# A Swin block with convolution on one core: shorter norm on VectorE, ScalarE's x1 copies moved up, other MLP banks, GpSimd's x1 rows ahead of the shifts

## The reference

```python
def _layer_norm(x, g, b):
    mu = x.mean(-1, keepdims=True)
    var = ((x - mu) ** 2).mean(-1, keepdims=True)
    return (x - mu) / jnp.sqrt(var + EPS) * g + b
...
xn = _layer_norm(x, ln1_g, ln1_b)
xs = jnp.roll(xn, shift=(-SHIFT, -SHIFT), axis=(1, 2))
...
qkv = wins @ qkv_w + qkv_b
attn = softmax(q * scale @ k.T + bias + mask)   # per window and head
out = roll_back(windows_back(attn @ v) @ proj_w + proj_b)
x = shortcut + out
y = _layer_norm(x, ln2_g, ln2_b)
y = jax.nn.gelu(y @ fc1_w + fc1_b)
x = x + (y @ fc2_w + fc2_b)
...
y = depthwise3x3(relu(x)) + dw_bias
y = (y @ pw_kernel + pw_bias) * inv + (beta - moving_mean * inv)
```

## Time and profile before

| | |
|---|---|
| median of 3 runs | 5511.71 us (5501.87 to 5517.33) |
| the profiled execution, its own time | 5513.41 us |
| its span | 5511.6 us |
| busy PE, DVE, ACT, POOL | 96%, 94%, 92%, 70% of the span |
| mean busy share of the DMA engines | about a tenth; 39 GB/s |
| granted clock of TensorE, over the span | 0.995 of full speed |
| chain that ended last, by engine | DVE 37%, POOL 28%, PE 23%, ACT 6%, issue 5% |

### The profile page before, as it was taken

The page is one execution under the profiler, slowest core; times in us unless marked ns, Lnnn a source line. Parts: engine busy times, 40 slices in busy tenths (PEclk is TensorE's granted clock), DMA queues, the critical chain, the costliest instruction groups (busy, mean ns, idle before and its releaser), DMA issues.

```text
span 5511.6 us, 202651 instructions
## 1 busy us (share of the span) xinstructions
PE 5283.0 (96%) x81186; PEld 3763.1 (68%) x81186; DVE 5190.1 (94%) x13517; ACT 5061.2 (92%) x10782; POOL 3841.7 (70%) x4105
## 2 busy tenths in 40 slices
PE   5999999999999999999999999999999999999998
PEld 3666666666666666666666666666666766666665
DVE  4999999999999999999999999999999999999998
ACT  4999999999998999999999999999999999999996
POOL 3677777777776777777777777777776777777773
PEclk9999999999999999999999999999999999999998
DMA  1111111111111111111111111111111111111111
GB/s 26 38 39 40 39 40 40 40 40 41 40 39 38 41 38 41 40 39 40 39 40 40 40 40 41 40 39 40 39 40 39 40 40 41 39 41 40 39 40 27
DMA packets 304318, 216.10 MB, mean 39 GB/s; under 512 B 233255, under 2 KB 274712, under 8 KB 303384
## 3 DMA queue, kind: packets, MB, share of 16 engines
q1 hardware_dynamic: 303384, 203.13, 13.9%
HBM read 77.81 MB, written 77.07 MB: 28 GB/s over the span
## 4 chain that ended last, share of the span: by engine, by line
DVE 37%; POOL 28%; PE 23%; ACT 6%; issue 5%; SPq 1%; DVEq 0%; DMA 0%; POOLq 0%; ACTq 0%
DVE acc L873 13%; PE bank L441 12%; POOL prob L985 11%; POOL prob L976 11%; POOL x1n L1002 6%; DVE stats L891 5%; DVE smax L841 5%; DVE prob L832 5%; DVE x L928 4%; PE bank L549 4%; ACT xT L685 3%; ACT x1T L638 3%; PE bank L478 3%; PE bank L424 1%; PE bank L459 1%
## 5 line engine op out<-in xcount | busy, mean ns | idle before, releaser
L873 DVE SCALAR_TENSOR_TENSOR acc<-ymap,taps,acc 96x784 f32<-96x784 f32 (+2 forms) x2176 | 2157.9, 996 | 54.8
L991 POOL TENSOR_TENSOR rstd<-var_eps,minus_half 112x7 f32<-112x7 f32 x512 | 936.2, 1828 | 1091.5 <-DVE var_eps L906 1091.5
L441 PE MATMUL bank<-x1T,w 96*128 96x448 f32 (+1 forms) x3072 | 1136.5, 506 | 87.2 <-ACT x1T L638 85.9
L976 POOL TENSOR_TENSOR prob<-prob,smax 128x392 f32<-128x392 f32 x768 | 829.4, 1080 | 430.3 <-DVE smax L841 430.3
L459 PE MATMUL bank<-hT,w 128*96 128x448 f32 (+1 forms) x3072 | 1097.9, 493 | 0.0
L649 ACT ACTIVATE hT<-bank,bfc 128x448 f32<-128x448 f32 (+1 forms) x1536 | 826.0, 575 | 54.9 <-PE bank L441 36.0
L1002 POOL TENSOR_SCALAR xn<-x_in,minus_mean,rstd 112x96 f32<-112x96 f32 x768 | 834.5, 1096 | 45.2 <-POOL offset L994 45.1
L441 PEld LDWEIGHTS bank<-x1T,w 96*128 96x128 f32 x3072 | 545.4, 191 | 411.2 <-issue 193.6
L459 PEld LDWEIGHTS bank<-hT,w 128*96 128x96 f32 x3072 | 466.9, 163 | 342.8 <-issue 166.0
L985 POOL TENSOR_TENSOR prob<-prob,srec 128x392 f32<-128x392 f32 x768 | 630.6, 848 | 0.4 <-DVE srec L850 0.4
L703 ACT ACTIVATE ymap<-bank,cols 96x448 f32<-96x448 f32 (+4 forms) x544 | 494.3, 921 | 73.3 <-PE bank L459 73.3
(11 more groups left out here) (101 smaller groups left out, 10464.0 us busy)
## 6 DMA issues: line engine op xcount, KB each, us to landing
out<-o_tile SPq DMA_DIRECT2D x256, 210.0 KB, 2.5
x_in<-in_x SPq DMA_DIRECT2D x256, 168.0 KB, 2.9
x_in<-in_x SPq DMA_DIRECT2D x256, 126.0 KB, 2.8
k<-qk SPq DMA_DIRECT2D x512, 49.0 KB, 1.9
ymap<-ymap SPq DMA_DIRECT2D x256, 85.5 KB, 2.0
out<-o_tile SPq DMA_DIRECT2D x256, 84.0 KB, 2.5
hT<-in_L_conv_rel_bias SPq DMA_DIRECT2D x49, 0.6 KB
x1T<-in_L_conv_fc_w SPq DMA_DIRECT2D x1, 144.0 KB, 2.4
```

The lines of the kernel that those rows point to most:

```text
L441: pe.matmul(bank[(1, 2, 5)[m]][:, 0:n * PT_], w1[:, m * 128:(m + 1) * 128], x1T[:, first * PT_:(first + n) * PT_], start=True, stop=True). ...
L873: last = dve.scalar_tensor_tensor(out=dst, in0=src, scalar=taps[:, i:i + 1], in1=dst, op0=ALU.mult, op1=ALU.add)
L976: pool.tensor_tensor(p, p, m, ALU.subtract).then_inc(shifted, 1)
L991: pool.tensor_tensor(b["rstd"][:], b["var_eps"][:], minus_half[0:PT_], ALU.pow)\
```

## The change

The norm: DVE keeps four of its seven small instructions (difference, deviation with the epsilon, between, and their sum `squares`), scaled by C throughout, and the factor sqrt(C) that this leaves goes into the weights, once, ahead of the loop. POOL takes over the sum of the halves' means and minus the mean, behind the statistics (`stats_done`), ahead of its root. The rows that POOL normalises are now x times rstd plus offset. ACT copies x1T ahead of the second xT copy. `hidden` writes banks 2, 5, 1 in turn, and its waits move along with them. POOL normalises its x1n rows ahead of the shifts.

```diff
@@ hidden, TensorE
                     if i == 0:
+                        wait(pe, x1t_ready, nth(t - 1, 2, 0))
+                    elif i == 1:
+                        wait(pe, x1t_ready, nth(t - 1, 2, 1))
+                    elif i == 2:
                         wait(pe, xt_ready, nth(t + 2, 2, 1))
-                    elif i == 1:
-                        wait(pe, x1t_ready, nth(t - 1, 2, 0))
                     elif i > 2:
                         wait(pe, h_ready, nth(t - 1, 6, i - 3))
-                    pe.matmul(bank[(1, 2, 5)[m]][:, 0:n * PT_], w1[:, m * 128:(m + 1) * 128],
+                    pe.matmul(bank[(2, 5, 1)[m]][:, 0:n * PT_], w1[:, m * 128:(m + 1) * 128],
@@ step, ScalarE
                 probs_turned(t + 1, 2)
+                x1_turned(t + 1)
                 x_turned(t + 1, 1)
-                x1_turned(t + 1)
                 attention_out(t + 1)
@@ norm_stats, VectorE
-                dve.tensor_tensor(b["sum"][:], st[:, :, 1], st[:, :, 4], ALU.add)
                 dve.tensor_tensor(b["diff"][:], st[:, :, 1], st[:, :, 4], ALU.subtract)
-                dve.tensor_tensor(b["dev"][:], st[:, :, 2], st[:, :, 5], ALU.add).then_inc(parts_done[which], 1)
+                dve.scalar_tensor_tensor(out=b["dev"][:], in0=st[:, :, 2], scalar=C * LN_EPS, in1=st[:, :, 5],
+                                         op0=ALU.add, op1=ALU.add).then_inc(parts_done[which], 1)
                 wait(dve, parts_done[which], nth(s, 1, 0))
-                dve.tensor_scalar(b["minus_mean"][:], b["sum"][:], -0.5, None, ALU.mult)
-                dve.scalar_tensor_tensor(out=b["between"][:], in0=b["diff"][:], scalar=0.25, in1=b["diff"][:],
-                                         op0=ALU.mult, op1=ALU.mult)
-                dve.tensor_scalar(b["within"][:], b["dev"][:], 1.0 / C, eps, ALU.mult, ALU.add)\
-                    .then_inc(halves_done[which], 1)
+                dve.scalar_tensor_tensor(out=b["between"][:], in0=b["diff"][:], scalar=0.25 * C, in1=b["diff"][:],
+                                         op0=ALU.mult, op1=ALU.mult).then_inc(halves_done[which], 1)
                 wait(dve, halves_done[which], nth(s, 1, 0))
-                dve.tensor_tensor(b["var_eps"][:], b["between"][:], b["within"][:], ALU.add)\
+                dve.tensor_tensor(b["squares"][:], b["between"][:], b["dev"][:], ALU.add)\
                     .then_inc(ln_ready[which], 1)
@@ root and rest, GpSimd
+                wait(pool, stats_done[which], nth(s, 1, 0))
+                pool.tensor_tensor(b["sum"][:], b["stats"][:, :, 1], b["stats"][:, :, 4], ALU.add)\
+                    .then_inc(summed[which], 1)
+                wait(pool, summed[which], nth(s, 1, 0))
+                pool.tensor_scalar(b["minus_mean"][:], b["sum"][:], -0.5, None, ALU.mult)
                 wait(pool, ln_ready[which], nth(s, 1, 0))
-                pool.tensor_tensor(b["rstd"][:], b["var_eps"][:], minus_half[0:PT_], ALU.pow)\
+                pool.tensor_tensor(b["rstd"][:], b["squares"][:], minus_half[0:PT_], ALU.pow)\
...
-                    last = pool.tensor_scalar(dst[:, j], src[:, j], b["minus_mean"][:, j:j + 1],
-                                              b["rstd"][:, j:j + 1], ALU.add, ALU.mult)
+                    last = pool.tensor_scalar(dst[:, j], src[:, j], b["rstd"][:, j:j + 1],
+                                              b["offset"][:, j:j + 1], ALU.mult, ALU.add)
@@ step, GpSimd
                 second_scale(t)
+                second_rest(t)
                 shift(t + 1, 0)
                 shift(t + 1, 1)
                 shift(t + 1, 2)
-                second_rest(t)
```

More of the change, by code:

```diff
@@ L50 @@
 LN_EPS, BN_EPS = 1e-4, 1e-3
+ROOT_C = float(C) ** 0.5
 MASKED = -100.0
@@ L158, in swin_conv_kernel @@
                (("stats", (WS, 6)), ("sum", (WS,)), ("diff", (WS,)), ("dev", (WS,)), ("between", (WS,)),
-                ("within", (WS,)), ("minus_mean", (WS,)), ("var_eps", (WS,)), ("rstd", (WS,)),
-                ("offset", (WS,)))} for i in (1, 2)]
+                ("squares", (WS,)), ("minus_mean", (WS,)), ("rstd", (WS,)), ("offset", (WS,)))} for i in (1, 2)]
         bank = [ctx.enter_context(nc.psum_tensor(f"bank{i}", [128, 512], F32)) for i in range(8)]
@@ L195, in swin_conv_kernel @@
         rstd_done = [sem("rstd1_done"), sem("rstd2_done")]
+        summed = [sem("summed1"), sem("summed2")]
         scale_ready = [sem("scale1_ready"), sem("scale2_ready")]
@@ L648, in gelus @@
                     wait(act, h_psum, nth(t - 1, 6, i))
-                    act.activation(hT[:, m, first * PT_:(first + n) * PT_], bank[(1, 2, 5)[m]][:, 0:n * PT_],
+                    act.activation(hT[:, m, first * PT_:(first + n) * PT_], bank[(2, 5, 1)[m]][:, 0:n * PT_],
                                    ACT.Gelu_apprx_tanh, bias=bfc1[:, m:m + 1]).then_inc(h_ready, 1)
@@ L780, in _ @@
                     if kind == "q":
-                        dve.tensor_scalar(to, qkv_raw[:, at:at + HD], cols[:, 0:1], SCALE, ALU.mult, ALU.mult)
+                        dve.tensor_scalar(to, qkv_raw[:, at:at + HD], cols[:, 0:1], SCALE * ROOT_C, ALU.mult, ALU.mult)
                     else:
-                        dve.tensor_scalar(to, qkv_raw[:, at:at + HD], cols[:, 0:1], None, ALU.mult)
-            dve.tensor_scalar(wk12[:], qkv_raw[:, C + HD:2 * C], cols[:, 0:1], None, ALU.mult)
-            dve.tensor_scalar(wv[:], qkv_raw[:, 2 * C:], cols[:, 0:1], None, ALU.mult).then_inc(dve_set, 1)
+                        dve.tensor_scalar(to, qkv_raw[:, at:at + HD], cols[:, 0:1], ROOT_C, ALU.mult, ALU.mult)
+            dve.tensor_scalar(wk12[:], qkv_raw[:, C + HD:2 * C], cols[:, 0:1], ROOT_C, ALU.mult, ALU.mult)
+            dve.tensor_scalar(wv[:], qkv_raw[:, 2 * C:], cols[:, 0:1], ROOT_C, ALU.mult, ALU.mult).then_inc(dve_set, 1)
             dve.wait_ge(pe_set, 2)
             dve.tensor_tensor(proj_row, bank[3][0:1, 0:C], proj_b_row, ALU.add).then_inc(dve_set, 1)
-            dve.tensor_scalar(w1[:], w1_raw, cols[:, 2:3], None, ALU.mult).then_inc(dve_set, 1)
+            dve.tensor_scalar(w1[:], w1_raw, cols[:, 2:3], ROOT_C, ALU.mult, ALU.mult).then_inc(dve_set, 1)
             dve.tensor_scalar(var_eps, cols[:, 7:8], BN_EPS, None, ALU.add).then_inc(dve_set, 1)
@@ L885, in values, with norm_stats @@
                                 bank[6 + i][:, 0:4 * C]).then_inc(v_ready[i], 1)
-            def norm_stats(which, s, src, eps):
+            def norm_stats(which, s, src):
                 b = ln[which]
@@ L916, in norm_x @@
                 wait(dve, x_loaded[slot], 32 * (s // UNROLL + 1))
-                norm_stats(0, s, x_in[:, slot], LN_EPS)
+                norm_stats(0, s, x_in[:, slot])
             def add_x(t, phase):
@@ L930, in add_x @@
                 wait(dve, x1_ready, nth(t, 2, 1))
-                norm_stats(1, t, x1[:, t % 2], LN_EPS)
+                norm_stats(1, t, x1[:, t % 2])
             def step(t, phase):
```

## The result

The changed kernel takes 5377.81 us in the median (5374.79 to 5381.52, 4 runs), beside 5513.55 us for the kernel before (5501.87 to 5517.33, 4 runs): a ratio of 0.9755, 95% interval 0.9742 to 0.9767. That is 136 us less, where 109 were forecast (5403), inside the range of 5335 to 5485. The profiled execution has a span of 5379.7 us, 131.9 less than before.

The account below looks back on a forecast made before the run. No engine is full; a ring of waits through POOL, PE and ACT bounds a 20.93 us strip. Afterwards a ring through the first gelu sums to 20.50, saving 0.43 x 254 = 109 us: 5403 us, range 5335 to 5485.

Parts of the forecast that it names:

- The ring that closes over POOL: POOL's shifts, x1n rows, divisions, then PE and ACT copies; moving the rows removes PE's 0.16 wait without delaying shifts.
- The shorter norm: Three of DVE's seven small instructions go, 0.24 a norm, plus 0.50 waiting for POOL; DVE busy 20.15 to 19.17.
- POOL's two new instructions cost DVE nothing: POOL's sum and minus the mean, after the statistics: DVE cost between nothing and 0.50, taken as nothing.
- The gelu ring: Second `hidden` through PE, ACT's copies and first gelu to the next second `hidden`: closes at 20.50 us a strip.
- The sum: Whole kernel: a strip falls from 20.93 to 20.50 us, 0.43 saved, times 254 gives 109 us.
- the 31 us of strips with something extra: Strips longer than the ordinary 20.93 us: 255 x 0.12 = 31 us over the run, assumed unchanged.
- PE runs free: Rival: ACT reaches the first gelu 0.3 earlier, only PE bounds, strip 20.1, 5300 us; chance 0.11.
- DVE held up: Rival: POOL's new small instructions delay DVE 0.50 a norm, strip 20.8, 5479 us; chance 0.15.
- the rows meet the taps: Rival: POOL's moved x1n rows take 3.35 beside DVE's taps and delay the shifts, 5715 us; chance 0.07.
- The gelu ring is longer: Rival: ACT's copies behind the third probT copy don't move up, 0.3 of 0.43 lost, 5480 us; chance 0.09.

Follow-up runs that it names:

- the ring opened: The change, but the second `hidden` writes banks 4, 0 and 2 in place of 2, 5 and 1: 5280.98 us, ratio 0.9580.
- opened ring without the norm: The change with the second `hidden` on banks 4, 0, 2 and without the shorter norm: 5327.99 us, ratio 0.9664.
- the banks alone: The kernel before with the second `hidden` on banks 4, 0, 1 and nothing else: 5511.00 us, ratio 0.9992.

## Why the prediction was right, and where it was off

- *The ring that closes over POOL.* Right. With the rows moved, PE's wait for the divisions is gone (42.1 us to 1.5), and the shifts aren't delayed: the first one still waits 0.39 for its maximum.
- *The shorter norm, 0.24 and 0.50 off DVE, and none of it in the sum.* Right. DVE's busy time per strip went from 20.15 to 19.26, where 19.17 was forecast. From its first small instruction to the tap behind it, the norm of x1 takes 0.60 where it took 0.80, that of x 0.62 where it took 1.33: 0.20 and 0.71 less, not 0.24 and 0.74. The ordinary strip is the same without the shorter norm.
- *POOL's two new instructions cost DVE nothing.* Right: 0.21 and 0.26 beside DVE's four at 0.17 to 0.19. The rule of the Trainium skill ("SBUF — State Buffer", section "SBUF: two separate sides") would allow a delay here of up to 0.2 for each. The rows don't agree with it for instructions this short: POOL's sum (2716.12 to 2716.33) runs at the same time as `diff` (2716.07 to 2716.24), which has two inputs and takes its usual 0.17. A `dev` longer by 0.03 is the most that they can hold.
- *The gelu ring, 20.50 us.* Right in mechanism and in size: 20.54 measured. PE waits 0.23 for the first gelu, where 0.3 was said. Work put into the ring moves the strip one for one, work behind it doesn't, and with the ring opened the strip falls to 20.09. Term by term, the near match holds errors that cancel. The rows after:

```profile
2718.97 1.02 ACT L673 COPY attnT<-bank 96x224 f32<-96x224 f32 x2
...
2722.00 3.26 ACT L652 ACTIVATE hT<-bank,bfc 128x448 f32<-128x448 f32 x6
...
2735.51 0.55 PE L526 MATMUL bank<-ident,xn 112*96 112x112 f32 x4
...
2736.15 0.93 ACT L688 COPY xT<-bank 96x448 f32<-96x448 f32 x1
2736.89 1.44 ACT L660 COPY probT<-bank 113x452 f32<-113x452 f32 x3
...
2739.50 1.02 ACT L673 COPY attnT<-bank 96x224 f32<-96x224 f32 x2
```

From the second `hidden` (2722.76) to the end of the first transposes it is 13.30 (13.36 was said, with the 0.10 for having waited), then 0.09 and 0.74 as said. From the first probT copy to attnT it is 2.61 (2.70), from attnT to the gelu 3.03 (2.95), and from the gelu to `hidden` 0.76 (0.66).

- *The sum, 0.43 x 254 = 109 us.* This is the term that was mis-sized. The ordinary strips give 0.40 x 254 = 101, and the rest of the gain lies in strips that the prediction left out. The step that failed is the sentence on the 31 us of strips with something extra, "which I leave as they are". From the sixth first-gelu to the 251st, 245 strips, the kernel before takes 5159.5 and the changed one 5043.9 us: 115.6 less, of which 97 or so are ordinary (0.397 x 245). The other 18 come in the main from two kinds of strip. At an image's edge (every 16th strip) each tap and map copy is two instructions. Such a strip took 21.43 and now takes 20.55, 0.88 less and not 0.40: 7 us for 15 strips. It took 21.45 with the copies alone, 21.04 with the norm alone and 20.94 with the x1n rows alone, which points to DVE's load as what it paid for. The second kind is TensorE's holes ahead of `weigh_values` (below), some 12 us.
- *The ends of the run.* The last 16 us of the 131.9 lie in the first and last strips (9.1 ahead of the stretch, 7.2 behind it), where 10 strips at 0.4 would have given 4. Most of the rest is TensorE's clock, which the prediction doesn't have. In the profiled execution before, it was granted at half (0.50, the level of 1.2 GHz) from 189.6 to 199.8 us and from 5449.5 to 5463.2; in the one after, not at all ahead of the stretch and only from 5324.1 to 5327.5 behind it. A stretch of 10.2 us at half clock made its strip 4.7 us longer (below), so by estimate this is some 9 us. Both executions have one more such stretch in their middle strips, where the two nearly cancel.
- *The rivals.* "PE runs free" did not happen, and needed another edit to happen; the 20.1 it was priced at was then met (20.09), though its last 0.3, put to weight loads, had no row behind it. "DVE held up" and "the rows meet the taps" are out, by the rows above. (The prediction says there that DVE's maxima and sums read PSUM; by the rows they read `prob`, and only the bias add reads a bank. The shifts keep their 0.85 beside them all the same.) "The gelu ring is longer" is out too: ACT waits for nothing from its xT copy to the gelu.

## What to carry to other kernels

When all engines are nearly full, add up rings, not busy times: start at a wait, follow start to start through whoever releases it until the same instruction of the next round, and do it again with that ring cut, since the next one sets what an edit is worth. Then see in the trace who waits for whom: a sum can come near with the wrong ring, as it did here for the copies alone and for the change without the x1n rows' move. An edit can be worth nothing alone and much beside another (the banks: 0 on the kernel before, 97 us on the changed one; the norm: about 8 us in one place, 47 in another). Look separately at the rounds that differ from the ordinary one; slack on an engine pays there even where it pays nothing elsewhere.

## What the runs showed of the hardware

**Holes ahead of small matmuls.** Once in some 18 strips, PE pauses ahead of `weigh_values` without waiting for any engine. A packet of the instruction queue q8 had started 2.2 to 3.2 us before PE went on, in each such pause of the four traces compared (before, after, x1n rows alone, and opened ring without the norm). In the kernels in which PE waits for the divisions in the step before it, the pauses are long: 16.2 us in 15 times before, 16.2 in 14 with the norm alone, 14.3 in 12 with the copies alone, 14.4 in 14 without the move, 16.1 in 13 with the banks alone. In most of the others they are short: 5.8 us in 12 times with the x1n rows alone, 5.4 in 15 without the copies, 6.6 in 11 without the norm, 3.7 in 14 in the change, 2.0 in 5 with the ring opened. But with the ring opened and without the norm they are long again, 15.3 us in 15 times, and PE waits for no divisions there. So that wait isn't what makes them long, or not it alone; the cause is open.

**TensorE's clock after a long pause.** Between the start and the last strips, the clock fell to half in 16 places of the 14 traces, each time during or within 2.1 us after a pause of PE of 1.2 to 2.7 us. In the kernel before that is a pause of 1.73 that ends at 1686.33, in the change one of 1.44 that ends at 2220.41. The windows view of the stretches behind them has the granted clock third from the end, 0.50 of full speed:

```profile
1688.00:1698.30 10.30, 10.30 (x30) 6.77 (x29) 6.33 (x20) 6.64 (x16) 3.54 (x3) 0.50 0.10 29
```

```profile
2221.50:2231.60 10.10, 10.10 (x30) 6.58 (x29) 5.91 (x17) 4.94 (x11) 3.80 (x5) 0.50 0.11 33
```

The strip with it was 4.7 us longer than the median one before, and 6.1 after, where the pause of 1.44 lies in the same strip. Not each such pause did it: one of 1.75 without the move left the clock at full. The kernels with short pauses have few of these stretches: none with the x1n rows alone, without the copies, or with the ring opened, against two before and four each with the norm alone and the copies alone.

**A VectorE instruction waited to the end of a GpSimd one.** A small instruction with two inputs took 0.67 next to a division of 392 columns and ended with it (2740.09 and 2740.08), and 0.17 once the division was out of the way. In two kernels that leave the x1n rows behind the shifts it is still 0.66 (copies alone) and 0.68 (without the move); the same kind of instruction wasn't held by GpSimd's sum over 7 columns (0.17 to 0.19).

**ScalarE's small instructions under the end of a copy.** Three activations of one element took 0.38 but moved the table load behind them by 0.13, since the load starts only when what is ahead of it has ended, and without them that was the copy (0.28 long, load 0.31 after its start).
